# Inverse roots of the keys on GpSimd, and cells and token rows in another order, in a two-layer attention and expert kernel

## The chip, the cores and the metric

The kernel runs on one core of a Trainium2 chip. The metric is the device time of one execution in microseconds (us). Engines are TensorE (PE in the profile, its weight loads PEld), VectorE (DVE), ScalarE (ACT), GpSimd (POOL) and SyncE (SP, which issues most transfers). Everything is float32 unless a row says otherwise.

## The reference, cut to what matters

The input is 8 batches of 256 tokens of 512 values. Layer 0 has attention and a mixture of experts, layer 1 an adapted linear map and a second mixture; each layer adds its result to its input.

```
q, k, v = x @ Wq.T, x @ Wk.T, x @ Wv.T        # 8 query heads, 4 key/value heads, 64 wide
q, k = rope(rms(q, q_scale), pos), rope(rms(k, k_scale), pos)   # rms: x * rsqrt(mean(x*x) + 1e-6) * (1 + scale)
k_blocks, v_blocks = ... .at[block, :, off].set(k), ...set(v)   # new rows go into a paged pool
p = softmax(q @ k_all.T / 16, over the last 256 positions)
y = (p @ v_all) @ Wo.T
# experts of layer 0: one dense matrix W, plus sparse changes for each of 8 experts
deltas   = softmax(expert_atom_weights) @ atoms          # 8 x 4096
weighted = deltas * sigmoid(importance)
vals     = sum over the top 2 experts of rw * weighted   # each of 4096 values belongs to a cell mask_idx of the 512x512 matrix
out      = y @ W.T + segment_sum(y[:, cols] * vals, rows)
```

Layer 1 (a linear map with LoRA adapters, then 8 experts with GELU) is untouched by the change.

## The kernel before, in words

The program is written out by hand, engine by engine; each engine has one queue of instructions in program order and waits on semaphores. There are 16 tiles of 128 tokens, two to a batch.

**Key stage and opening.** TensorE projects tile after tile of x to 256 key and 256 value columns into PSUM bank t mod 8 (line 673) and may reuse a bank once ScalarE has read it out (`kv_nr`). ScalarE squares the keys head by head with a sum (`squares`, line 968). For each pair of tiles VectorE (`sums_k`, line 1376) makes the mean, its reciprocal, ScalarE takes the square root (`roots`, line 973), and VectorE does one Newton step to get `rstd` (last line 1390). ScalarE scales the keys by it and copies the values (`scaled`, lines 981 and 983), VectorE applies the rope (`rope_k`, lines 1397, 1400, 1409), SyncE stores the tile in `new_kv` (line 363). Between the pairs VectorE works on the page tables (`index_work`, lines 1281 to 1372). GpSimd fetches raw weights (lines 505 to 509), then waits for the index of the first batch and for all 16 stores, gathers the rows of batch 0 from the pool (`old_rows`) and from `new_kv` (`new_rows`, line 524, `over_rows`, line 552), and makes the query scales (`scales`, lines 531 to 544): an inverse root by a bit trick and three Newton steps, 15 small operations with a drain after each.

TensorE behind the keys projects query tile 0 into bank 0, multiplies raw weights with the gates (lines 807 to 815), projects query tile 1 into bank 0, forms `deltas` with 128 records on 8 columns into banks 6 and 7 (line 823), turns the query tile and the two halves of the keys (line 679) through bank 0, each copied by ScalarE before the next, and waits for the cell weights of VectorE (`wgt_ok`) and for the weights w_o and w0 (`att_w`). Then the batches begin.

**Batches.** A period of batch B has 8 steps j. TensorE does scores of two (head, tile) pairs (`dots`, line 704), turns probabilities of the pair before (`turn_p`, line 711) and mixes values (`mix`, line 723); it projects queries of the next batch at j = 2 and 4, turns keys of the next batch at j = 6 and 7, and between these projects the attention output. VectorE masks and takes maxima (`tops`, line 1505), scales probabilities (line 1516), ropes the next queries, and routes finished tokens. Bank 0 is shared by all such uses in a fixed order (`uses`), with counters `bk` (written) and `bc` (read out). In batch 0 `cell_sums` (line 743) adds cells that have the same index, and VectorE's `move_cells` takes the sums.

**Cells.** The sparse changes are scattered with an add into `m_buf`, 32 scatters one after the other (`cells`, line 566), 8 each in rounds b = 1 to 4 of GpSimd's loop (line 585). The same loop gathers rows of batch b + 1, makes its query scales, and sends token rows of finished batches to the experts' buffer (`send`, line 558). SyncE fetches `m_buf` back in 16 pieces into two buffers (`fetch_m`, line 371), the first two after the second query projection of batch 5 and after all 32 scatters; VectorE adds them to the dense matrix (`add_cells`, line 1534), one half piece in each step from j = 3 of batch 5 on. After batch 7 the additions left over are done, then both layers' experts run.

The cell values need `atoms`, which lie where the rows of batch 1 go; so GpSimd waits for `delta` before it gathers those.

## Time and profile before

| | us |
|---|---|
| median of 3 runs | 1119.12 (1115.15 to 1119.79) |
| the profiled execution | 1120.77 |
| its span, first to last instruction | 1119.0 |
| TensorE busy | 944.0 (84%) |
| VectorE busy | 556.6 (50%) |
| ScalarE busy | 418.8 (37%) |
| GpSimd busy | 329.0 (29%) |
| mean granted TensorE clock | 0.932 of full speed |

Times in rows are microseconds from the span's start, lengths of one instruction in a group are ns. In a timeline a row has start, length, engine, line, operation, what it writes and reads, how often, and in brackets the idle time of its engine just before and what ended it. SPq is SyncE's queue. A float32 product of TensorE shows as two records.

### The profile page before, as it was taken

Reading aid. Unit: us, or ns where it says so; the run is one execution under the profiler, and the core shown is the slowest. Engines: PE = TensorE matmul, PEld = TensorE weight load, DVE = VectorE, ACT = ScalarE, POOL = GpSimd, SP = SyncE. Lnnn points to the kernel's source line nnn. Section 1 sums busy time; section 2 is a strip of 40 time slices with the busy share of each in tenths; the row PEclk is TensorE's granted clock in tenths of the full one; section 3 lists DMA queues with packets and bytes.
Section 4 is the critical chain, followed back from the end, with each engine's and each line's share of the span. In section 5 each row is a group of like instructions: output and inputs, shape, how many; then the busy total and the mean of one; then the engine's idle time right before and its main releaser. Section 6 shows DMA issues by size and latency. Waiting matters only on the chain.

```text
span 1119.0 us, 18432 instructions
## 1 busy us (share of the span) xinstructions
PE 944.0 (84%) x4690; PEld 609.2 (54%) x4691; DVE 556.6 (50%) x2242; ACT 418.8 (37%) x1283; POOL 329.0 (29%) x368
## 2 busy tenths in 40 slices
PE   6995799888986798706989996999199999999994
PEld 2463475454543454403434444888077777777772
DVE  4678757675753878563333442455333333333331
ACT  3452645554543555301111111222144444555440
POOL 3003215646553152111333441133212212212221
PEclk9986989999999899967999998999689999999998
DMA  8947314244234243357777774794643333333330
GB/s 283 301 189 256 106 39 127 66 115 118 69 87 133 78 137 132 114 167 213 205 209 158 136 125 132 283 395 170 195 113 63 67 67 69 69 67 68 61 58 1
DMA packets 76552, 152.12 MB, mean 136 GB/s; under 512 B 15719, under 2 KB 24599, under 8 KB 74832
## 3 DMA queue, kind: packets, MB, share of 16 engines
q1 hardware_dynamic: 38624, 84.87, 23.0%
q0 software_dynamic: 25520, 45.11, 19.7%
q10 hardware_dynamic: 12352, 21.51, 5.8%
q8 instruction: 20, 0.33, 0.1%
q14 instruction: 36, 0.29, 0.1%
HBM read 94.05 MB, written 69.00 MB: 146 GB/s over the span
## 4 chain that ended last, share of the span: by engine, by line
PE 62%; DVE 11%; DMA 10%; issue 9%; ACT 3%; DVEq 2%; SPq 1%; another core or an unknown queue 1%; POOL 0%; ACTq 0%; POOLq 0%
PE ps L657 50%; DMA acc<-R,tok_i 5%; PE ps L663 4%; PE ps L723 3%; DVE R L1516 2%; DVE R L1534 2%; PE ps L711 2%; DVE R L1505 1%; ACT R L1011 1%; DMA R<-acc 1%; DMA R<-rows 1%; PE ps L704 1%; DMA rows<-zrow 1%; DMA R<-m_buf 1%; PE ps L743 1%
## 5 line engine op out<-in xcount | busy, mean ns | idle before, releaser
L657 PE MATMUL ps<-R 128*128 128x128 f32 (+4 forms) x2768 | 689.3, 405 | 38.5 <-issue 19.6
L657 PEld LDWEIGHTS ps<-R 128*128 128x128 f32 x2768 | 421.2, 195 | 266.4 <-issue 251.2
L629 POOL DMA_INDIRECT out_x<-R,tok_i x39 | 60.5, 1551 | 252.5 <-DVEq L1859 156.9
L663 PE MATMUL ps<-ident,R 128*128 128x128 f32 x440 | 67.5, 286 | 75.0 <-DMA R<-rows 59.7
L663 PEld LDWEIGHTS ps<-ident,R 128*128 128x128 f32 x440 | 53.7, 147 | 108.9 <-issue 94.0
L1022 ACT ACTIVATE R<-R,nmx 128x384 f32<-128x384 f32 x128 | 78.3, 621 | 84.1 <-DVE nmx L1505 71.5
L558 POOL DMA_INDIRECT rows<-R,slot_i x64 | 65.0, 1015 | 141.0 <-DVEq L1608 62.9
L629 POOL DMA_INDIRECT acc<-R,tok_i x39 | 60.9, 1561 | 134.4 <-DVE R L1768 131.3
L1505 DVE CUSTOM_DVE_ANT_0 R<-ps,R,q_scale 128x384 f32<-128x384 f32 x128 | 73.6, 612 | 41.1 <-issue 41.1
L711 PE MATMUL ps<-ident,R 128*128 128x128 f32 x384 | 57.2, 285 | 34.3 <-DVE R L1516 22.6
L1181 ACT ACT_TABLE_LOAD x18 | 23.1, 1283 | 147.8 <-PE ps L657 147.8
L711 PEld LDWEIGHTS ps<-ident,R 128*128 128x128 f32 x384 | 43.6, 145 | 60.1 <-DVE R L1516 34.9
L1173 ACT ACTIVATE R<-R 128x2048 f32 x39 | 75.4, 1937 | 1.5 <-issue 1.5
L1854 DVE TENSOR_TENSOR R<-ps,R 128x512 f32<-128x512 f32 x39 | 27.0, 691 | 95.9 <-PE ps L657 95.9
L1106 ACT ACTIVATE R<-ps 128x512 f32<-128x512 f32 x39 | 23.3, 597 | 108.8 <-PE ps L663 103.4
L566 POOL DMA_INDIRECT m_buf<-tot,cell_i x32 | 51.4, 1605 | 37.2 <-DMA m_buf<-tot,cell_i 21.8
L704 PE MATMUL ps<-R 64*128 64x384 f32 x256 | 61.3, 559 | 0.8 <-ACT R L999 0.8
L1028 ACT ACTIVATE R<-ps 128x384 f32<-128x384 f32 x128 | 56.5, 506 | 5.9 <-PE ps L711 5.9
L1516 DVE TENSOR_SCALAR R<-R,rsum 128x384 f32<-128x384 f32 x128 | 49.4, 427 | 5.6 <-issue 0.9
L1181 ACT ACTIVATE R<-ps,inv_f 128x128 f32<-128x128 f32 x156 | 44.6, 377 | 18.4 <-PE ps L657 18.2
L723 PE MATMUL ps<-R 128*64 128x256 f32 x384 | 51.0, 403 | 0.0
L1834 DVE COPY R<-ps 128x512 f32<-128x512 f32 x39 | 25.3, 686 | 51.1 <-PE ps L663 51.1
(292 smaller groups left out, 901.0 us busy)
## 6 DMA issues: line engine op xcount, KB each, us to landing
R<-rows SPq DMA_DIRECT2D x78, 258.0 KB, 3.1
R<-in_fc ACTq DMA_DIRECT2D x16, 1024.0 KB, 5.6
m_buf<-R SPq DMA_DIRECT2D x8, 1024.0 KB
R<-m_buf SPq DMA_DIRECT2D x16, 512.0 KB
R<-acc SPq DMA_DIRECT2D x32, 256.0 KB
R<-in_x_t SPq DMA_DIRECT2D x4, 1024.0 KB, 10.9
R<-in_x_t SPq DMA_DIRECT2D x8, 512.0 KB, 3.6
new_kv<-R SPq DMA_DIRECT2D x16, 256.0 KB, 2.0
```

The source lines that it names most:

```text
L558: po.indirect_dma_start(out=rows_d, out_offset=bass.IndirectOffsetOnAxis(ap=slot_i[:, c, t:t + 1], axis=0), in_=rows[:, t, :], in_offset=N ...
L629: po.indirect_dma_start(out=sums[s], out_offset=bass.IndirectOffsetOnAxis(ap=tok_i[:, s:s + 1], axis=0), in_=y_sb[s], in_offset=None, boun ...
L657: m = pe.matmul(out, lhs(k), rhs(k), start=(k == 0 and first), stop=(k == KC - 1 and last))
L663: m = pe.transpose(out[:, k * P:(k + 1) * P], src[:, k * P:(k + 1) * P], ident[:])
L704: pe.matmul(ps[:, 2 + u % 4, 0:KW], q_t[s][base:base + 64, jj, qt * P:(qt + 1) * P], k_t[s][base:base + 64, p, qt * P:qt * P + KW], start= ...
L711: m = pe.transpose(ps[:, 6 + u % 2, c * P:(c + 1) * P], prob[u % 4][:, c * P:(c + 1) * P], ident[:])
L723: n = pe.matmul(ps[HD * x:HD * (x + 1), 1, KC // 2 * P * (m % 2):KC // 2 * P * (m % 2 + 1)].rearrange("p (i q) -> p i q", q=P), kv[s][:, q ...
L1022: ac.activation(prob[u % 4], msk_s[u % 4], ACT.Exp, bias=nmx[:, u:u + 1], scale=-1.0, accum_out=sums[:, u:u + 1]).then_inc(S["s_exp"], 1)
L1173: ac.activation(fc1_s[s], fc1[:, :, e, :], ACT.Copy).then_inc(S2["k_w"][s], 1)
L1181: g = ac.activation(h_t[s][:, c, :], ps[:, 2 + s, c * P:(c + 1) * P], ACT.Gelu, bias=b1_t[:, e, c:c + 1])
L1505: ve.tensor_tensor_reduce(out=msk_s[u % 4], in0=ps[:, 2 + u % 4, 0:KW], in1=mask[:, u // NH, :], scale=q_scale[:, B % 2, u:u + 1], scalar= ...
L1516: TS(prob[u % 4], prob[u % 4], rsum[:, u % NH:u % NH + 1], None, ALU.mult).then_inc(S["s_sc"], 1)
```

## The change

1. Keys' roots: `sums_k` and `roots` are gone. GpSimd makes `rstd` for a pair of tiles (`key_roots`) with the same steps as the query scales (`inverse_roots`, 14 operations). ScalarE squares one pair ahead of the pair that it scales; `ss` and `rstd` have four slots instead of two.
2. GpSimd's queue: pairs 0 and 1 stand ahead of the raw-weight transfers, pairs 2 to 7 ahead of everything else, with the gathers of batch 0's old rows behind pair 5.
3. Query tile 1 is projected straight behind query tile 0, into bank 2; the two key turns of the opening go to banks 3 and 4.
4. The 128 records of `deltas` move from the opening to the first two steps of batch 0 (bank 1), VectorE's cell weights to step 1 of batch 0. The wait for w_o and w0 moves to batch 1.
5. VectorE's `index_work` and `sparse_eq` are spread in another way over the key stage.
6. GpSimd's loop over batches: three scatters go ahead of the scales, three go between the row transfers behind them. SyncE asks for the first two pieces of `m_buf` after the stores of batch 4 instead of after the second query projection of batch 5.

```diff
@@ SyncE
-            sp.wait_ge(S["bk"], uses(-1)["p1"] + 1)
+            sp.wait_ge(S["o_p1"], 1)
             load_q(1)
...
                     load_q(b + 2)
-                if b == 5:
-                    sp.wait_ge(S["mscat"], 16 * ST)
-                    for m in range(2):
-                        fetch_m(m)
                 sp.wait_ge(S["s_pv"], 4 * b + 2)
                 sp.dma_start(a0[b], x0[b]).then_inc(S["acc_z"], 16)
...
+                if b == 4:
+                    sp.wait_ge(S["mscat"], 16 * ST)
+                    for m in range(2):
+                        fetch_m(m)
@@ GpSimd
+            def inverse_roots(src, out, k):
+                x, y, t = nw_x[:, 0:k], nw_y[:, 0:k], nw_t[:, 0:k]
+                po.tensor_scalar(x, src, 1.0 / HD, RMS_EPS, ALU.mult, ALU.add)
+                po.drain()
+                po.tensor_scalar(y.bitcast(I32), x.bitcast(I32), -0.5, 1597463007.0, ALU.mult, ALU.add)
+                po.drain()
+                for n in range(3):
+                    po.tensor_tensor(t, y, y, ALU.mult)
+                    po.drain()
+                    po.tensor_tensor(t, t, x, ALU.mult)
+                    po.drain()
+                    po.tensor_scalar(t, t, -0.5, 1.5, ALU.mult, ALU.add)
+                    po.drain()
+                    po.tensor_tensor(out if n == 2 else y, y, t, ALU.mult)
+                    if n < 2:
+                        po.drain()
+            def key_roots(n):
+                r = slice(2 * (n % 2), 2 * (n % 2) + 2)
+                po.wait_ge(S["kv_sq"], 2 * n + 2)
+                wait(po, S["kv_nr"], 2 * n - 2)
+                inverse_roots(ss[:, r].rearrange(flat), rstd[:, r].rearrange(flat), 2 * NG)
+                po.drain().then_inc(S["rst"], 2)
+            for n in range(2):
+                key_roots(n)
             po.wait_ge(S["w_kv"], 16)
...
-            po.wait_ge(S["idx_ok"], 1)
-            old_rows(0)
+            for n in range(2, NT // 2):
+                key_roots(n)
+                if n == 5:
+                    po.wait_ge(S["idx_ok"], 1)
+                    old_rows(0)
...
-            po.wait_ge(S["delta"], 1)
+            po.wait_ge(S["delta"], 2)
             old_rows(1)
...
+                if add:
+                    for n in range(2, 5):
+                        cells(t + n)
+                if b + 1 < NB:
+                    scales(b + 1)
                 for n in range(4):
                     if b >= 2:
                         ...
                         send(a_rows, 2 * b - 4 + n // 2, n % 2, S["xs_sc"])
-                    if add:
-                        cells(t + 2 + n)
-                if b + 1 < NB:
-                    scales(b + 1)
-                if add:
-                    cells(t + 6)
-                    cells(t + 7)
+                    if add and n < 3:
+                        cells(t + 5 + n)
@@ TensorE
+            def cell_deltas(x):
+                if x == 0:
+                    pe.wait_ge(S["pre_c"], 1)
+                    pe.wait_ge(S["atoms_d"], 32)
+                for t in range(ST // 2 * x, ST // 2 * (x + 1)):
+                    for y in range(2):
+                        m = pe.matmul(ps[64 * y:64 * y + 64, 1, t * NE:(t + 1) * NE], ...)
+                m.then_inc(S["delta"], 1)
...
+                    if j == 0 and first:
+                        pe.wait_ge(bc, uses(-1)["q0"] + 1)
+                        pe.wait_ge(S["o_kc"], 2)
+                        pe.wait_ge(S["q_rp"], 2)
...
+                        if B == 1:
+                            pe.wait_ge(S["att_w"], 16 * (2 * KC + 1))
...
                     dots(B, j, s)
+                    if j < 2 and first:
+                        cell_deltas(j)
...
             project_q(opening, 0)
+            pe.wait_ge(S["kv_nr"], NT - 5)
+            queries(1, 2).then_inc(S["o_p1"], 1)
             pe.wait_ge(S["raw_dma"], 16 * 5)
-            pe.wait_ge(S["kv_nr"], NT - 6)
...
-            project_q(opening, 1)
...
             for p in range(2):
-                turn_k(opening, p, 0)
-            pe.wait_ge(S["wgt_ok"], 1)
-            pe.wait_ge(S["att_w"], 16 * (2 * KC + 1))
+                turn_k4(ps[:, 3 + p, :], 0, p).then_inc(S["o_k"], 1)
@@ ScalarE
+            for t in range(2):
+                squares(t)
+            for n in range(NT // 2):
+                for t in (2 * n + 2, 2 * n + 3):
+                    if t < NT:
+                        squares(t)
+                for t in (2 * n, 2 * n + 1):
+                    scaled(t)
@@ VectorE
+            for n in range(NT // 2):
                 for x in range(2):
                     rope_k(2 * n + x)
+                if n in (0, 1, 2, 3, 4):
+                    next(index)
+                if n in (2, 4):
+                    next(index)
+                if n == 5:
+                    tables(0, tabq_a, tabq_b)
+                if n == 6:
+                    sparse_eq(0, 4)
...
             rope_q(0)
-            sparse_eq(0, 8)
             rope_q(1)
             outside(0)
             build_mask(0)
-            cell_weights()
+            sparse_eq(4, 8)
```

## Rows read from the trace of the kernel before

**Rows 1.** The chain of waits, opening; start, length, what.

```profile
82.28 13.62 issue
95.90 5.79 PE ps L657 x8
101.69 7.16 PE ps L823 x126
```

**Rows 2.** Timeline of TensorE, key stage and opening.

```profile
10.73 60.64 PE L657 MATMUL ps<-R 128*128 128x512 f32 x136 [10.73 <-DMA R<-in_x_t]
...
110.67 1.09 PE L679 MATMUL ps<-ident,R 128*128 128x128 f32 x4 [0.78 <-ACT R L999]
...
114.34 2.93 PE L704 MATMUL ps<-R 64*128 64x384 f32 x8 [0.78 <-ACT R L999]
...
118.93 0.88 PE L711 MATMUL ps<-ident,R 128*128 128x128 f32 x6 [1.06 <-DVE R L1516]
```

**Rows 3.** Timelines of ScalarE and VectorE, first squares and last keys.

```profile
19.75 0.20 ACT L968 ACTIVATE R<-ps 128x64 f32<-128x64 f32 x1
...
88.14 0.93 ACT L981 ACTIVATE R<-ps,rstd 128x64 f32<-128x64 f32 x4 [1.02 <-DVEq L1391]
...
87.91 0.16 DVE L1390 TENSOR_TENSOR rstd<-rstd,root 128x4 f32<-128x4 f32 x1
...
90.55 0.42 DVE L1409 TENSOR_TENSOR R<-R 128x256 f32<-128x256 f32 x1
```

**Rows 4.** Timeline of GpSimd, key stage and opening.

```profile
19.99 0.98 POOL L505 DMA_DIRECT2D gate<-in_gate_t  x1 [12.81 <-DMA R<-in_x_t]
...
23.22 0.78 POOL L509 DMA_DIRECT2D R<-in_b_o  x1
...
94.53 0.94 POOL L524 DMA_INDIRECT R<-new_kv,new_idx  x1 [44.05 <-DVEq L1371]
...
98.81 1.55 POOL L552 DMA_INDIRECT R<-new_kv,new_idx  x1 [0.30 <-issue]
...
105.67 0.60 POOL L533 TENSOR_SCALAR nw_y<-nw_x 128x16 int32<-128x16 int32 x1 [1.48 <-issue]
...
112.03 0.27 POOL L544 TENSOR_SCALAR q_scale<-nw_y 128x16 f32<-128x16 f32 x1 [0.16 <-issue]
```

**Rows 5.** Timeline of GpSimd, batches 4 and 5.

```profile
314.81 0.98 POOL L558 DMA_INDIRECT rows<-R,slot_i  x1 [0.30 <-issue]
316.19 1.58 POOL L566 DMA_INDIRECT m_buf<-tot,cell_i  x1 [0.40 <-DMA m_buf<-tot,cell_i]
...
320.99 0.29 POOL L533 TENSOR_SCALAR nw_y<-nw_x 128x16 int32<-128x16 int32 x1 [2.44 <-issue]
...
325.83 0.26 POOL L544 TENSOR_SCALAR q_scale<-nw_y 128x16 f32<-128x16 f32 x1 [0.16 <-issue]
...
330.28 1.56 POOL L566 DMA_INDIRECT m_buf<-tot,cell_i  x1 [1.65 <-DMA m_buf<-tot,cell_i]
...
372.15 0.98 POOL L536 TENSOR_TENSOR nw_t<-nw_y 128x16 f32<-128x16 f32 x1
```

**Rows 6.** Timeline of VectorE, batch 5.

```profile
372.02 1.09 DVE L1534 TENSOR_TENSOR R<-R 128x512 f32<-128x512 f32 x1
```

**Rows 7.** Timelines of VectorE and TensorE and the chain of waits, batch 5.

```profile
363.18 1.07 DVE L1534 TENSOR_TENSOR R<-R 128x512 f32<-128x512 f32 x1 [13.43 <-DMA R<-m_buf]
...
364.88 1.54 PE L711 MATMUL ps<-ident,R 128*128 128x128 f32 x6 [7.20 <-DVE R L1516]
...
358.13 5.02 DMA R<-m_buf
```

**Rows 8.** Timeline of SyncE's queue, the stores of batches 4, 5 and 6.

```profile
321.17 0.52 SPq L393 DMA_DIRECT2D acc<-in_x  x1
...
373.46 0.53 SPq L393 DMA_DIRECT2D acc<-in_x  x1
...
417.01 0.52 SPq L393 DMA_DIRECT2D acc<-in_x  x1
```

More of the change, by code:

```diff
@@ L117, in program @@
         nrm = [words(R2, 14336 + KD * s, [KD]) for s in range(2)]
-        sq = [words(R2, 14848 + KD * s, [KD]) for s in range(2)]
+        sq = [words(R2, base, [KD]) for base in (14848, 15104, 5120, 5376)]
         sin_t = words(R2, 15360, [NT, HD // 2])
@@ L206, in program @@
         tot = sb("tot", [P, ST, NE])
-        ss = sb("ss", [P, 2, NG])
-        rstd = sb("rstd", [P, 2, NG])
-        root = sb("root", [P, 2, NG])
+        ss = sb("ss", [P, 4, NG])
+        rstd = sb("rstd", [P, 4, NG])
         ssq = sb("ssq", [P, 16])
@@ L719, in mix @@
                     wait(pe, S["s_ot"], 2 * B + qt)
+                if B == 0 and m == 0:
+                    pe.wait_ge(S["wgt_ok"], 1)
                 for c in range(3):
@@ L963, in squares @@
             def squares(t):
[L964 removed]
                 ac.wait_ge(S["kv_mm"], t + 1)
[L966 removed]
+                wait(ac, S["rst"], 2 * (t // 2) - 2)
                 for h in range(NG):
[L968 removed]
+                    c = ac.activation(sq[t % 4][:, h * HD:(h + 1) * HD], ps[:, t % 8, h * HD:(h + 1) * HD], ACT.Square, accum_out=ss[:, t % 4, h:h + 1])
                 c.then_inc(S["kv_sq"], 1)
[L971 to L974 removed]
             def scaled(t):
[L977 to L978 removed]
+                ac.wait_ge(S["rst"], 2 * (t // 2) + 2)
                 wait(ac, S["p1r"], t - 1)
                 for h in range(NG):
[L981 removed]
+                    ac.activation(nrm[t % 2][:, h * HD:(h + 1) * HD], ps[:, t % 8, h * HD:(h + 1) * HD], ACT.Copy, scale=rstd[:, t % 4, h:h + 1])
                 wait(ac, S4["p1k"][t % 4], 16 * (t // 4))
                 ac.activation(kv_out[t % 4][:, KD:D], ps[:, t % 8, KD:D], ACT.Copy).then_inc(S["kv_nr"], 1)
[L985 to L994 removed]
+            for t in range(2):
[6 more added lines that the diff above has]
+                    scaled(t)
             bk, bc = S["bk"], S["bc"]
@@ L1077, in _ @@
             ac.activation(lora_b[:, D:DG], ps[:, 1, 128:128 + NE], ACT.Copy).then_inc(S["pre_c"], 1)
[L1078 removed]
             q_out(opening, 0, 0)
             for p in range(2):
[L1081 removed]
+                ac.wait_ge(S["o_k"], p + 1)
+                copy_bank(3 + p, k_t[0][:, p, :]).then_inc(S["o_kc"], 1)
             periods(ac, period)
@@ L1414, in rope_q @@
                 ve.wait_ge(S["q_ss"], t + 1)
-                rope(ps[:, 0, :], rq_a, rq_b, tabq_a, tabq_b, NH, t).then_inc(S["bc"], 1)
+                last = rope(ps[:, 2 if t == 1 else 0, :], rq_a, rq_b, tabq_a, tabq_b, NH, t)
+                if t != 1:
+                    last.then_inc(S["bc"], 1)
                 ve.drain()
@@ L1432, in _ @@
             next(index)
-            sums_k(0, 0, BOTH)
-            for n in range(NT // 2 - 1):
-                if n < 6:
-                    next(index)
-                if n == 6:
-                    tables(0, tabq_a, tabq_b)
-                if n + 1 < NT // 2 - 1:
-                    sums_k(n + 1, 2 * n + 2, BOTH)
-                else:
-                    sums_k(n + 1, NT - 2, (0,))
+            for n in range(NT // 2):
                 for x in range(2):
                     rope_k(2 * n + x)
-            sums_k(NT // 2, NT - 2, (1,))
-            for x in range(2):
-                rope_k(NT - 2 + x)
-            next(index)
+                if n in (0, 1, 2, 3, 4):
[6 more added lines that the diff above has]
+                    sparse_eq(0, 4)
             def cell_weights():
@@ L1669, in period @@
                         build_mask(1)
+                    if j == 1 and first:
+                        cell_weights()
                     if j == 2 and not last:
```

96 lines of the change are left out of this document (25 added, 71 removed).

## The prediction

> **What bounds the kernel now.** I read the chain of waits first, then the timelines of the engines in the opening, then the waits of the batches. Up to 71 us TensorE is never idle: 136 records of key and query products run back to back [rows 2], so nothing that speeds up the keys' normalisation can shorten that part. What the other engines owe at its end is the price. TensorE has done the products of the raw weights at 82.28 and then stands for 13.62 us [rows 1]: the second query projection wants bank 0, which VectorE frees only after the ropes of all keys, and these trail. The last inverse root is ready at 87.91 + 0.16 = 88.1, the last key is roped at 90.97 [rows 3], GpSimd starts its four gathers of new rows at 94.53 [rows 4]. From there everything is serial: projection, cell products (7.2 us), turns of the queries and keys through one bank, first scores at 114.34, first turned probabilities at 118.93 [rows 1, 2]. A second hole is in batch 5: VectorE waits 13.43 us for the first piece of `m_buf`, since SyncE asks for it only after the second query projection of that batch; TensorE is idle for 7.20 us in it [rows 7]. Behind batch 7 (experts, layer 1) the change touches no instruction.
>
> **Step 1, the key stage with its roots on GpSimd.** Before, each pair went ScalarE, VectorE, ScalarE (root), VectorE, with VectorE's index work in the same queue. Now VectorE and ScalarE give up their part (9 times six VectorE and one ScalarE instructions of about 0.2 us; this pays nothing in itself, TensorE covers it), and GpSimd has 14 small operations with drains per pair. A quiet run of the same code is 13 intervals from 320.99 to 325.83, 0.37 us each [rows 5], so a pair costs c = 14 x 0.37 = 5.2 us when nothing disturbs it. The disturbed run in the opening took from 105.67 to 112.30 for 14 operations, 6.6 us [rows 4]. I take c = 5.8, since VectorE's ropes of two SBUF operands fill roughly half of the time.
> GpSimd's queue is now in this order: pairs 0 and 1, the five raw-weight transfers (19.99 to 24.0, 4.0 us [rows 4]), pairs 2 to 5, two gathers (half of the four that took 94.53 to 100.36 [rows 4], 2.9), pairs 6 and 7. After a transfer the first drain costs: the second operation comes 3.2 us after the last issue ended (317.77 to 320.99 [rows 5]). That is twice 3.2. The first pair can begin when its eight squares of 0.20 are there, 19.75 + 1.6 = 21.3 [rows 3]. So the last roots are ready at R = 21.3 + 8c + 4.0 + 2.9 + 6.4 = 34.6 + 8c: 76.2 for 5.2, **81.0 for 5.8**, 87.4 for 6.6. TensorE is not held up by it: its last key product needs pair 3, the first query projection pair 4, the second pair 5, and these are ready more than 5 us earlier at c = 5.8. Raw weights asked for some 13 us later are still wanted only at 75 us.
>
> **Step 2, from R to the first probabilities.** Scaling tile 14 on ScalarE takes 0.93 and a copy, 1.2 [rows 3]; the two ropes run 2.7: stored at R + 3.9. From there to the gathers 3.6 (90.97 to 94.53 [rows 3, 4]), four gathers 5.8: R + 13.3. Then the query scales: 3.2 for the first drain, 5.1 for the rest [rows 5]: R + 21.6 is where VectorE can start on scores. The squares of both query tiles no longer hold them, because the second projection now runs at 71 to 75, into bank 2, at the rate of the key products (8 of 136 records in 60.64 us, 3.6) instead of the 5.79 at 95.90 [rows 1, 2]. Beside that TensorE: the last gather lands about 1.7 after its issue (as a scatter does, 1.65 [rows 5]), R + 15.0; two key turns of 1.1 into two banks and one copy of 0.8 [rows 2]: R + 18.0. Then, new on this path, the cell products: scores 1.5, half of 7.2, scores 1.5, the other half, a query turn 1.0 [rows 1, 2]: the first probabilities are turned at **R + 29.2**. The scales at R + 21.6 hide behind that. Before it was 118.93. So the opening gives 89.7 - R: **8.7 us** at c = 5.8, 13.5 at 5.2, 2.3 at 6.6. Of the rest, VectorE's cell weights move behind the products that they need, its eight comparisons are split four before and four after the last ropes (I price them with the spread of c), and SyncE's 1 MB weight transfer, waited for only in batch 1, is off the path. Rows for batch 1 are gathered later relative to batch 0, after the cell products, but are wanted in its step 6, some 35 us on.
>
> **Step 3, the fetch moved from batch 5 to the end of batch 4.** SyncE issues two transfers of 512 KB after the stores of batch 4 (321.17 [rows 8]) as soon as all 32 scatters are in; behind that wait stands only the last query load, which follows a projection of batch 5 that was over at 357.7 (the end of what the fetch waited for [rows 7]). In GpSimd's new order three scatters go before the scales and three after, between the row transfers. In the times of before: scales done at 326.1, a row transfer of 1.0 with a gap of 0.3, then three scatters at 3.3 each, the other row transfers in their shadow: the last one lands at about 338.3 (before 331.8 + 1.6 [rows 5]). The first piece takes 5.0 from issue [rows 7]: 343.3, against 349.75 when VectorE asks for it (363.18 - 13.43 [rows 7]). Six us of margin, so the wait goes. It isn't worth its 13.43: TensorE was partly ahead. The mark of the stores tells: batch 4 to 5 took 52.29 us, batch 5 to 6, with more additions in it, 43.55 [rows 8]. **8.7 us.** Ends: 6.0 (TensorE's idle time less the gap of about a us that is there in other batches) and 13.4. What is late next is the ordinary pace of a batch, VectorE with additions and scales.
> The scales of the next batch are nowhere later: they wait for the squares at 318.35 (320.99 less 2.44 and 0.20) in either order [rows 5]. Token rows go out after them, and are wanted only after batch 7.
>
> **Sum.** The profiled execution took 1120.8 (span 1119.0). 1120.8 - 8.7 - 8.7 = 1103.4. The median of the runs shown, 1119.1, lies 1.7 lower, so I say **1102**.
>
> **Rivals.**
> GpSimd and VectorE get in each other's way. In batch 5 a GpSimd product of normally 0.22 us lasted 0.98, from 372.15 to 373.13, and VectorE's addition of two SBUF operands ran from 372.02 to 373.11 [rows 5, 6]: it ended with it. If each of the 14 operations waits out one rope instruction of 0.42 [rows 3], c = 5.2 + 5.9 = 11.1, R = 123.4, the opening loses 33.7, and the time is 1120.8 + 33.7 - 8.7 = 1146. Slower by over 0.5% needs R above 104, c above 8.7. For it: the same engines are now busy in the same stage. Against: ropes are in bursts with waits between, and of the batches' scale runs most operations were undisturbed. 4 in 100. The Trainium skill (SBUF — State Buffer, SBUF: two separate sides) says that the pair of ports which both engines use is locked exclusively for a whole instruction when VectorE has two SBUF inputs; by that rule as the full case c would be near 11 and the sum 1146; the trace agrees on the lock and not on its happening each time.
> The middle of it: c about 6.6, the roots end where they ended before, the opening gives only 2. Then 1120.8 - 2.3 - 8.7 = 1109.8, or 1108 by the median. 13 in 100.
> The opening is better: drains after transfers cost little and c = 5.2. The floor of R is the last squares, one projection ahead of TensorE's 71.4 and 0.9 more, so 69, and 5.2: 74, a gain of 15.7; with c = 5.2 alone it is 13.5. At 15, 1120.8 - 15 - 8.7 = 1097, 1095 by the median. 13 in 100.
> The scatters are late, because rows share their queue, and VectorE still waits in batch 5: only the opening's 8.7 is left, 1112, 1110 by the median. Against it the six us of margin. 7 in 100.
> Neither does what it says, a gather or a store that lands late under the weight transfers takes the place of the roots, and batch 5 hides its hole otherwise: 1119. 4 in 100.
> My forecast, both steps within their bounds, has 59 in 100.
>
> **The numbers.** About 0.5%, 5.6 us, is what a measurement of this kernel tells from no change; 1113.5 is that bound. Forecast, the middle case, the better opening and most of the late-scatter case lie below: 0.90. Same 0.06, slower 0.04. Range: the forecast's ends (8.7 by 2.3 to 13.5, 8.7 by 6 to 13.4) and the neighbouring rivals give 1093 to 1112.
>
> **What would show it.** In the profile after: TensorE without a gap over 2 us up to 75, last ropes near 85 instead of 91; GpSimd's runs of 14 operations at 5 to 6.5 us; probabilities first turned near 110; cell products between the first scores; in batch 5 no wait of VectorE for `m_buf`, and 43 to 45 us between the stores of batches 4 and 5. Wrong if a GpSimd run takes over 7 us, if TensorE waits in the key stage, if the chain in batch 0 passes through a gather of batch 1, or if everything from batch 1 on isn't the same length as before.

## The result, and the profile after

| | before | after |
|---|---|---|
| median of 8 runs each, side by side | 1118.01 us (1114.08 to 1119.79) | 1106.47 us (1102.52 to 1111.22) |
| span of the profiled execution | 1119.0 | 1104.9 |
| GpSimd busy | 329.0 | 358.8 |
| mean granted TensorE clock | 0.932 | 0.933 |

The ratio is 0.9911, interval 0.9886 to 0.9936: 11.5 us faster. The prediction said 1102 and 17 us. The total is in its range, but hardly a part of it came where it was put. The mark of SyncE's first store of each batch shows that; all marks of before stand in [rows 8] or in the same view (140.13 for batch 0, 188.71 for batch 1):

| stretch | before | after | gained |
|---|---|---|---|
| start to the stores of batch 0 | 140.13 | 151.18 | -11.05 |
| batch 0 to 1 | 48.58 | 48.35 | 0.23 |
| batch 1 to 4 (three batches) | 132.46 | 121.11 | 11.35 |
| batch 4 to 5 | 52.29 | 40.05 | 12.24 |
| batch 5 to the end | 745.54 | 744.21 | 1.33 |
| the whole span | 1119.0 | 1104.9 | 14.1 |

The opening, predicted to gain 8.7 us, lost 11. The fetch, predicted at 8.7, stands in a stretch that gained 12.2. And batches 1 to 4, priced at nothing, gained 11.4.

**The opening.** GpSimd's timeline of the kernel after, around its raw-weight transfers (start, length, and in brackets the idle time before):

```profile
33.70 0.20 POOL L516 TENSOR_TENSOR rstd<-nw_y,nw_t 128x8 f32<-128x8 f32 x1
35.98 0.99 POOL L534 DMA_DIRECT2D gate<-in_gate_t  x1 [2.08 <-issue]
...
39.24 0.77 POOL L538 DMA_DIRECT2D R<-in_b_o  x1
40.09 0.26 POOL L505 TENSOR_SCALAR nw_x<-ss 128x8 f32<-128x8 f32 x1
55.70 0.20 POOL L507 TENSOR_SCALAR nw_y<-nw_x 128x8 int32<-128x8 int32 x1 [15.36 <-issue]
```

The transfers of the same stretch (35 to 60 us: size, median us from issue to landing):

```profile
R<-in_w POOLq DMA_DIRECT2D x1, 1024.0 KB, 15.1
...
R<-in_b_o POOLq DMA_DIRECT2D x1, 256.0 KB, 16.1
```

The last transfer was issued at 39.24 and landed 16.1 us later, at 55.3; the drain between the first and second operation of pair 2 ended at 55.70. The timing fits a drain that waits until GpSimd's own transfers have landed (raw_sp, rows_behind and gather_first below test it); they share the DMA engines here with a megabyte of zeros and the stores. TensorE's timeline of the kernel after shows what hangs on that:

```profile
61.49 23.21 PE L678 MATMUL ps<-R 128*128 128x512 f32 x48 [7.28 <-ACT R L1017]
84.63 10.36 PE L678 MATMUL ps<-gate,R 128*64 128x8 f32 x104
94.92 0.27 PE L864 MATMUL ps<-ident,R 8*128 8x8 f32 x1
105.49 1.11 PE L684 MATMUL ps<-ident,R 128*128 128x128 f32 x4 [10.29 <-DVE R L1442]
115.83 1.94 PE L700 MATMUL ps<-ident,R 128*128 128x128 f32 x8 [9.23 <-DMA R<-new_kv,new_idx]
118.50 1.65 PE L729 MATMUL ps<-R 64*128 64x384 f32 x4 [0.73 <-issue]
120.08 3.69 PE L773 MATMUL ps<-eaw_t,R 64*64 64x8 f32 x64
...
129.82 1.49 PE L736 MATMUL ps<-ident,R 128*128 128x128 f32 x6
```

TensorE stands 7.28 us inside the key stage, which before had no gap [rows 2]: no bank was free, because no key could be scaled. The first probabilities are turned at 129.82; before it was 118.93. Further down GpSimd's queue:

```profile
84.03 0.22 POOL L507 TENSOR_SCALAR nw_y<-nw_x 128x8 int32<-128x8 int32 x1 [2.60 <-issue]
...
93.43 0.94 POOL L510 TENSOR_TENSOR nw_t<-nw_y 128x8 f32<-128x8 f32 x1
...
96.36 0.77 POOL L516 TENSOR_TENSOR rstd<-nw_y,nw_t 128x8 f32<-128x8 f32 x1
104.14 1.02 POOL L553 DMA_INDIRECT R<-new_kv,new_idx  x1 [7.00 <-DMA new_kv<-R]
...
116.01 0.21 POOL L507 TENSOR_SCALAR nw_y<-nw_x 128x16 int32<-128x16 int32 x1 [6.51 <-issue]
```

The last roots are ready at 97.13 (81.0 predicted); four operations of pair 7 took 0.76 to 0.94 instead of 0.20, beside VectorE's comparisons of cell indices; and the four gathers landed only 6.6 us after issue (the median; the last one took 7.6), so that the next drain took 6.51. TensorE's turn of the keys, which the landing of the last gather releases, starts at 115.83, and the operation behind the drain at 116.01. In the six kernels of "The opening, taken apart" these two stand 0.17 to 0.26 us apart as well.

**The fetch.** SyncE's timeline of the kernel after, batch 4 to 5 (before, the fetch stood behind the query projection of batch 5 and VectorE waited 13.43 us for it [rows 7]):

```profile
320.64 0.52 SPq L388 DMA_DIRECT2D acc<-in_x  x1
...
338.34 1.06 SPq L370 DMA_DIRECT2D R<-m_buf  x2
```

It goes out at 338.34, 17.7 us behind the mark of batch 4. The prediction had 338.3, which is 17.1 behind the mark of before. No wait of VectorE for `m_buf` is left in that batch.

### The profile page after: what moved, and what is told of

It reads as the page before. It is cut to its first block, busy times and chain, and to the rows that moved or that the text cites. A ratio compares the mean times of both kernels' runs of the same rounds, so it can differ in the third digit from the quotient of the medians.

```text
span 1104.9 us, 18551 instructions
## 1 busy us (share of the span) xinstructions
PE 936.2 (85%) x4690; PEld 607.2 (55%) x4691; DVE 546.7 (49%) x2188; ACT 415.6 (38%) x1273; POOL 358.8 (32%) x480
## 4 chain that ended last, share of the span: by engine, by line
PE 54%; DVE 13%; issue 12%; DMA 9%; POOLq 4%; DVEq 2%; ACT 2%; SPq 1%; POOL 1%; ACTq 0%
PE ps L678 43%; DMA acc<-R,tok_i 5%; PE ps L684 4%; PE ps L750 2%; DVE R L1534 2%; DVE R L1552 2%; DVE R L1523 2%; PE ps L736 1%; DMA R<-acc 1%; ACT R L1042 1%; DMA rows<-zrow 1%; PE ps L729 1%; DMA R<-rows 1%; PE ps L783 1%; DMA R<-new_kv,new_idx 1%
## 5 line engine op out<-in xcount | busy, mean ns | idle before, releaser
L678 PE MATMUL ps<-R 128*128 128x128 f32 (+4 forms) x2768 | 684.9, 404 | 23.3 <-DMA R<-in_x_t 10.5
L736 PE MATMUL ps<-ident,R 128*128 128x128 f32 x384 | 56.8, 283 | 22.8 <-DVE R L1534 12.2
L1144 ACT ACTIVATE R<-ps 128x512 f32<-128x512 f32 x39 | 23.3, 597 | 109.9 <-PE ps L684 107.6
L1031 ACT ACTIVATE R<-ps 128x512 f32<-128x512 f32 x48 | 28.5, 594 | 54.2 <-PE ps L684 39.5
```

The costliest lines, as they stand in the source:

```text
L678: m = pe.matmul(out, lhs(k), rhs(k), start=(k == 0 and first), stop=(k == KC - 1 and last))
L736: m = pe.transpose(ps[:, 6 + u % 2, c * P:(c + 1) * P], prob[u % 4][:, c * P:(c + 1) * P], ident[:])
```

## The experiments

Each ratio is to the kernel before, run beside it on the same chip; its median there was 1118 to 1126 us, so the ratios are what to compare. "Marks" are the stores of the batches, as in the table.

### One part of the change at a time

**fetch_only.** The kernel before with the move of the fetch alone:

```diff
-                if b == 5:
-                    sp.wait_ge(S["mscat"], 16 * ST)
-                    for m in range(2):
-                        fetch_m(m)
                 sp.wait_ge(S["s_pv"], 4 * b + 2)
                 sp.dma_start(a0[b], x0[b]).then_inc(S["acc_z"], 16)
...
+                if b == 4:
+                    sp.wait_ge(S["mscat"], 16 * ST)
+                    for m in range(2):
+                        fetch_m(m)
```

> The kernel before, with one edit: SyncE asks for the first two pieces of m_buf after the stores of batch 4 instead of in batch 5. Theory (the fetch gives what the prediction said): VectorE's wait of 13.43 us in batch 5 goes, the stores of batch 5 come 43 to 44 us after those of batch 4 instead of 52.3, and the time falls by 8 to 9 us. Rival (part of it was paid by other things, such as the faster batches of the changed kernel): it falls by less than 5. In both, batches 2 to 4 keep their 43.7 to 44.5 us each.

Measured: 1112.92 us, ratio 0.9894 (0.9855 to 0.9934). Batch 4 to 5 took 41.3 us instead of 52.29, batches 1 to 4 stayed at 43.1 to 43.9 each:

```profile
322.09 0.52 SPq L389 DMA_DIRECT2D acc<-in_x  x1
...
334.33 1.07 SPq L371 DMA_DIRECT2D R<-m_buf  x2
...
363.38 0.53 SPq L389 DMA_DIRECT2D acc<-in_x  x1
```

The fetch is worth 11.0 us by the marks.

**order_only.** The kernel before with the new order of GpSimd's loop alone:

```diff
+                if add:
+                    for n in range(2, 5):
+                        cells(t + n)
+                if b + 1 < NB:
+                    scales(b + 1)
                 for n in range(4):
...
-                    if add:
-                        cells(t + 2 + n)
-                if b + 1 < NB:
-                    scales(b + 1)
-                if add:
-                    cells(t + 6)
-                    cells(t + 7)
+                    if add and n < 3:
+                        cells(t + 5 + n)
```

> The kernel before, with one edit: GpSimd's loop has three scatters ahead of the query scales and the row transfers behind them. Theory A (the row transfers, or a transfer behind them, disturb TensorE in step 3 and 4 of batches 2 to 4, where it resumes 2.6 us late and then runs at half clock): batches 2 to 4 take 40 to 41 us each instead of 43.7 to 44.5, some 11 us less by batch 5, where VectorE's wait for m_buf stays, so the time falls by 9 to 12. Theory B (the batches of the changed kernel are faster for another reason, say the later opening): batches 2 to 4 stay at 44 and the time within 2 us.

Measured: 1109.67 us, ratio 0.9862 (0.9822 to 0.9902). Batches 1 to 4 at 40.70, 41.09 and 40.13 us: 10.5 us less than in before. Batch 4 to 5 stayed at 51.0. So the order of transfers, the part priced at zero, is worth about as much as the fetch: 10.5 against 11.0 us by the marks, and the intervals of the two ratios overlap.

**order_fetch.** Both, with the old opening.

> The kernel before with both of these edits and its old opening, so neither roots on GpSimd nor moved cell products. If the opening of the changed kernel costs what its trace shows (first probabilities turned at 129.8 against 118.9), this is some 11 us faster than the changed kernel: about 1096, 20 us or more under the kernel before. If the late opening is made up for later, it is within 3 us of the changed kernel.

Measured: 1097.74 us, ratio 0.975 (0.9704 to 0.9795). By the medians the two gains add up (15.1 and 11.9 against 27.1 us), the first probabilities come at 118.06, and this kernel, without the new opening, beats the changed one.

### What the order of transfers removes

Before, in batches 2 to 4, there is a stall that [rows 5] show only from GpSimd's side. TensorE and then ScalarE in batch 3 of the kernel before:

```profile
262.25 1.99 PE L657 MATMUL ps<-R 128*128 128x256 f32 x8
264.18 0.92 PE L704 MATMUL ps<-R 64*128 64x384 f32 x4
267.39 5.37 PE L657 MATMUL ps<-R 128*128 128x512 f32 x8 [2.29 <-issue]
```

```profile
266.86 0.38 ACT L1017 ACTIVATE R<-ps 128x256 f32<-128x256 f32 x1 [4.70 <-remote]
```

The same steps in order_only, TensorE and ScalarE:

```profile
261.20 1.99 PE L657 MATMUL ps<-R 128*128 128x256 f32 x8
263.12 0.92 PE L704 MATMUL ps<-R 64*128 64x384 f32 x4
263.97 3.70 PE L657 MATMUL ps<-R 128*128 128x512 f32 x8
```

```profile
263.23 0.38 ACT L1017 ACTIVATE R<-ps 128x256 f32<-128x256 f32 x1 [1.77 <-PE ps L657]
```

ScalarE reads the product 0.04 us behind its modelled end in order_only and 2.6 us behind it in before. VectorE, which waits for the scores, is late by about the same time (2.5 us). Then the query projection starts at the lower clock (granted 0.50 from 268 to 270, the 1.2 GHz level; 1.00 in order_only) and takes 5.37 instead of 3.70 us. Together 4.3 us in this batch (2.6 and 1.67); by the marks it is 3.5 per batch (44.15 on average in batches 1 to 4 against 40.64). In before the first row transfer of the round is issued at 261.34, 5.5 us ahead of ScalarE's late start. Three orders of the same ten transfers were tried on the kernel before.

**sends_behind.** The four scatters stay ahead of the scales, the four rows go behind them.

```diff
+                if add:
+                    for n in range(4):
+                        cells(t + 2 + n)
+                if b + 1 < NB:
+                    scales(b + 1)
                 for n in range(4):
...
                         send(a_rows, 2 * b - 4 + n // 2, n % 2, S["xs_sc"])
-                    if add:
-                        cells(t + 2 + n)
-                if b + 1 < NB:
-                    scales(b + 1)
```

> The kernel before; in GpSimd's loop the four scatters of the middle stay ahead of the query scales, and only the four transfers of token rows go behind the scales (before: row, scatter, row, scatter ... scales). Opening and fetch as before. Theory A (in batches 2 to 4 the token rows ahead of the scales, beside the scatters, go with the stall of 2.6 us and the slow query projection): the stores of batches 1 to 4 stand 40 to 41 us apart as in order_only, and the time is 8 to 13 us below before, ratio near 0.987. Rival B (it is the number of scatters ahead of the scales, three instead of four, that counts, or their landing): the stores stay 43 to 44.5 us apart and the time is within 3 us of before.

Measured: 1127.49 us, ratio 1.0043 (1.0029 to 1.0057). The stall is gone everywhere and batch 1 to 2 takes 40.86 us, as theory A says; but the next ones take 45.36 and 47.67. The trace suggests another reason. Four scatters in a row each wait for the landing of the one before, rows no longer fill that time, and with the rows and two scatters behind them the next round starts late. GpSimd's last operation of the scales in this kernel:

```profile
246.05 0.26 POOL L544 TENSOR_SCALAR q_scale<-nw_y 128x16 f32<-128x16 f32 x1 [0.16 <-issue]
```

That is 15.6 us behind the mark 230.41; in before it is 6.0 (239.18 against 233.17), in order_only 4.8.

**scatter_first.** Scatter and row change places in each of the four pairs.

```diff
                 for n in range(4):
+                    if add:
+                        cells(t + 2 + n)
                     if b >= 2:
...
                         send(a_rows, 2 * b - 4 + n // 2, n % 2, S["xs_sc"])
-                    if add:
-                        cells(t + 2 + n)
```

> The kernel before; in GpSimd's loop scatter and row transfer change places in each of the four pairs ahead of the scales (scatter, row, scatter, row ... instead of row, scatter, ...), so that the first row goes out some 3 us later in the batch. In before TensorE's signals to ScalarE and VectorE come 2.6 us late in batches 2 to 4 shortly behind the first row transfer, and the next query projection runs 5.36 instead of 3.70 us. Theory A (any token rows ahead of the scales bring the stall, wherever they stand): the stall is there again in batches 2 to 4, moved by up to 3 us or at the same step, stores 43.5 to 44.5 us apart, the time within 3 us of before. Rival B (it needs the row transfer at that very moment, beside a fetch of instructions at 217 or 261): the stall is gone in most batches, stores 40 to 41.5 apart, the time 6 to 12 us below before.

Measured: 1124.24 us, ratio 0.9996 (0.9968 to 1.0024). No stall of 2.6 us in batches 2 to 4, although rows still go ahead of the scales; every query projection takes 3.70. Batches 1 to 4 took 40.80, 45.64 and 40.92 us, batch 4 to 5 56.7. The gain is given back in the same way: 15.2 us behind the mark 231.63 the scales are ready, and VectorE's first masking of the batch (L1505) starts only then:

```profile
246.81 0.26 POOL L544 TENSOR_SCALAR q_scale<-nw_y 128x16 f32<-128x16 f32 x1 [0.16 <-issue]
```

```profile
247.17 0.61 DVE L1505 CUSTOM_DVE_ANT_0 R<-ps,R,q_scale 128x384 f32<-128x384 f32 x1 [2.07 <-issue]
```

**rows_alone.** The four rows ahead of the scales, all six scatters behind.

```diff
                         send(a_rows, 2 * b - 4 + n // 2, n % 2, S["xs_sc"])
-                    if add:
-                        cells(t + 2 + n)
                 if b + 1 < NB:
                     scales(b + 1)
                 if add:
-                    cells(t + 6)
-                    cells(t + 7)
+                    for n in range(2, 8):
+                        cells(t + n)
```

> The kernel before; ahead of the scales only the four row transfers, and all six scatters of the middle behind the scales. Theory A (the rows bring the stall): batches 2 to 4 show the late signals of 2.6 us and a projection over 5 us, the stores stay 43 to 44.5 us apart; time within 4 us of before. Rival B (the stall comes from scatters that alternate with rows): no stall, stores 40 to 41 us apart in batches 1 to 4. In both the scatters end later, so that the wait for m_buf in batch 5 may grow by a few us.

Measured: 1125.68 us, ratio 1.0021 (0.9989 to 1.0054), marks 43.67, 40.19 and 45.54 us apart. In rounds 2 to 4 of GpSimd's loop the late signals are back, now at another step, and in batch 3 to 4 the scales are late as well, 14.5 us behind the mark. The first row of batch 3's round is issued at 272.93, and ScalarE's timeline has:

```profile
279.06 0.60 ACT L997 ACTIVATE R<-ps 128x512 f32<-128x512 f32 x1 [5.20 <-remote]
```

Side by side, the late signals follow a pattern, but not without exception. In before a round's first row goes out directly behind the two gathers of `over_rows` (217.08, 261.34, 305.06, 347.14, 402.72), and 5.3 to 6.3 us later ScalarE's read starts (222.53, 266.86, 310.52, 353.47, 408.06): 2.5, 2.6 and 2.6 us behind the end of the product, then 1.9, and 1.2 in the last of the five:

```profile
408.06 0.38 ACT L1017 ACTIVATE R<-ps 128x256 f32<-128x256 f32 x1 [3.29 <-PE ps L657]
```

In fetch_only all five come again, 3.1 to 1.2 us late. In rows_alone it is 3.0 us in rounds 2 to 4 (in round 2 it is SyncE's store at 233.01 that comes 3.0 us behind the end of the product that it waits for), and none in rounds 5 and 6, though the rows stand there in the same way; in round 5 TensorE is idle at that time. scatter_first has a scatter between gathers and first row in rounds 2 to 4, and no signal 2.5 us late there. In rounds 5 and 6 no scatters are left, the row (350.28 and 404.14) stands behind the gathers, and the signal is 1.6 and 1.1 us late:

```profile
356.36 0.38 ACT L1017 ACTIVATE R<-ps 128x256 f32<-128x256 f32 x1 [3.71 <-remote]
```

But one in its round 4 is late too, by 1.2 us, and it comes ahead of that round's first row (310.92):

```profile
309.24 0.38 ACT L1017 ACTIVATE R<-ps 128x256 f32<-128x256 f32 x1 [3.27 <-PE ps L657]
```

sends_behind, order_only, order_fetch and after never have a row directly behind the gathers, and at this step no signal more than 0.6 us late. So the long delays go with such a row in every case, and short ones come without it. That the row is their cause isn't shown, and what the signal waits for was not found: fetches of instructions stand near the rows in both kinds of kernels.

So two things go with the order. A first row directly behind the gathers goes with 3.5 us lost in a batch by the marks. Scales 14.5 to 17.2 us behind the mark go with some 5 us or more, while at 11.8 and 12.2 a batch took 40.9 us as in order_only. The new order avoids both; sends_behind and scatter_first run into the second and rows_alone into both.

### The opening, taken apart

Each kernel is the one above it with one more edit, and all have the new order and fetch.

**raw_sp.** The kernel after, the five raw-weight transfers asked for by SyncE.

```diff
@@ SyncE, behind the load of mask_bc
+            sp.dma_start(gate0[:], d["gate0_t"].rearrange(chunked, p=P)).then_inc(S["raw_dma"], 16)
...
+            sp.dma_start(raw_b, d["b_o"].rearrange(chunked, p=P)).then_inc(S["raw_dma"], 16)
@@ GpSimd, behind pair 1
-            po.wait_ge(S["w_kv"], 16)
...
-            po.dma_start(raw_b, d["b_o"].rearrange(chunked, p=P)).then_inc(S["raw_dma"], 16)
```

> The changed kernel with one edit: the five raw-weight transfers go out from SyncE's queue, behind the mask indices, instead of from GpSimd's. Theory (a GpSimd drain stands until the transfers of its own queue have landed): the gap of 15.4 us behind the first operation of pair 2 is gone, the pairs follow each other at 5 to 6.5 us, TensorE doesn't wait before 71 us, the last root is ready at 76 to 82 instead of 97.1, first probabilities are turned at 110 to 115 instead of 129.8, and the time is 14 to 20 us below the changed kernel. Rival (the gap comes from the load on the transfer engines or from VectorE): a gap of over 8 us stays and so does the time, within 4 us.

Measured: 1102.23 us, ratio 0.9817 (0.9763 to 0.9871), first probabilities at 123.13 instead of 129.82. Pair 2 starts at 35.12 and runs through; the gap of 15.4 us is gone, as the theory said. But the last roots are ready only at 90.94 (76 to 82 expected) and the first probabilities come 6.7 us earlier, not 15 to 20. ScalarE now waits 9.71 us, to 52.44, for a store that stands behind the raw weights in SyncE's queue, and pair 4 waits for ScalarE. The next gap of the same kind, behind the gathers of old rows, remains too:

```profile
55.63 0.20 POOL L510 TENSOR_SCALAR nw_x<-ss 128x8 f32<-128x8 f32 x1 [8.93 <-ACT R L1004]
...
73.13 0.45 POOL L510 TENSOR_SCALAR nw_x<-ss 128x8 f32<-128x8 f32 x1
78.56 0.20 POOL L512 TENSOR_SCALAR nw_y<-nw_x 128x8 int32<-128x8 int32 x1 [4.99 <-issue]
```

**rows_behind.** The old rows of batch 0 behind pair 7 instead of pair 5.

```diff
             for n in range(2, NT // 2):
                 key_roots(n)
-                if n == 5:
-                    po.wait_ge(S["idx_ok"], 1)
-                    old_rows(0)
+            po.wait_ge(S["idx_ok"], 1)
+            old_rows(0)
```

> The kernel after, raw weights from SyncE's queue (as in raw_sp), and the two gathers of batch 0's old rows behind pair 7 of the key roots instead of between pairs 5 and 6. Theory A (a drain behind a transfer of GpSimd's own queue waits until that transfer has landed): in raw_sp the second operation of pair 6 came 4.99 us after the first; here pair 6 has no such gap, the last roots are ready near 86 instead of 90.94, and the first drain behind the gathers comes with the query scales, where one is paid anyway. Time 2 to 5 us below raw_sp (ratio near 0.978). Rival B (the gap is the cost of a new kind of instruction, or of waiting for ScalarE): pair 6 keeps a gap of 4 us or more and the time is raw_sp's, 0.982. Rival C: the gap goes, but VectorE's index work or the stores hold the last keys, so that the gathers start where they started (97.9) and the time is the same.

Measured: 1096.81 us, ratio 0.976 (0.9726 to 0.9794). No gap in pair 6, the last roots at 81.99, first probabilities at 114.76. The roots come 9 us earlier than in raw_sp, not 5: with the drain's 4.99 the two issues and GpSimd's wait of 2.98 us ahead of them left the chain. The mark of batch 0 comes 8.6 us earlier (144.76 to 136.13); the intervals of the two ratios overlap a little.

**gather_first.** SyncE asks for w_o, w0 and the last zeros only when batch 0 is gathered.

```diff
+            sp.wait_ge(S["o_p1"], 1)
+            load_q(1)
             sp.wait_ge(S["pre_w"], 1)
+            sp.wait_ge(S2["kvd"][0], 64)
             for k in range(KC):
```

> The kernel rows_behind, and SyncE asks for the weights w_o and w0 and for the last zero stores only when the gathers of batch 0 have landed (they are not needed before batch 1; the load of the next queries goes ahead of them). Theory A (the gathers land late because the weights and zeros share the DMA engines; 6.6 us median in the kernel after): the gathers land 2 to 3 us after issue, the second operation of the query scales comes 2 to 3 us after the first instead of 6, TensorE's key turns start 3 to 4 us earlier relative to the gathers' start, and the time is 3 to 4 us below rows_behind. Rival B (the gathers' time is that of the gathers themselves, four of 128 rows one after the other): landing stays above 5 us, the time stays.

Measured: 1090.04 us, ratio 0.9682 (0.9658 to 0.9706). The drain in the scales fell from 4.99 to 1.60 us, TensorE's wait for the gathers from 7.62 to 4.23, first probabilities at 111.54. By the mark of batch 0 the step is worth 3.0 us (136.13 to 133.15); the two ratios, whose intervals don't overlap, differ by more (0.976 and 0.9682).

**eq_late.** VectorE's first four comparisons moved from behind pair 6 to the end of the opening.

```diff
-                if n == 6:
-                    sparse_eq(0, 4)
...
             build_mask(0)
-            sparse_eq(4, 8)
+            sparse_eq(0, 8)
```

> The kernel gather_first, and VectorE's first four comparisons of cell indices moved from behind the ropes of pair 6 to the end of the opening, where the other four stand. Theory A (they hold the ports that GpSimd shares: its products took 0.94, 0.80, 0.76 and 0.77 beside them instead of 0.20): pair 7's roots take 5 us instead of 7.8, the last roots come 2 to 3 us earlier, and the time is 2 us below gather_first unless the comparisons, now 7.6 us together, hold the first scores. Rival B (the long products come from the ropes or from ScalarE's reads): pair 7 keeps products of 0.7 us or more and the time is the same or longer.

Measured: 1086.68 us, ratio 0.967 (0.965 to 0.969). GpSimd's same two operations in pair 7, in gather_first and in eq_late:

```profile
78.16 0.93 POOL L522 TENSOR_TENSOR nw_y<-nw_y,nw_t 128x8 f32<-128x8 f32 x1
79.23 0.79 POOL L516 TENSOR_TENSOR nw_t<-nw_y 128x8 f32<-128x8 f32 x1
```

```profile
77.18 0.20 POOL L522 TENSOR_TENSOR nw_y<-nw_y,nw_t 128x8 f32<-128x8 f32 x1
77.53 0.20 POOL L516 TENSOR_TENSOR nw_t<-nw_y 128x8 f32<-128x8 f32 x1
```

The comparisons made them long. Now seven operations of the query scales last 0.74 to 0.80 beside all eight comparisons, but TensorE's cell products cover that: first probabilities at 108.04.

**raw_spread.** The raw weights go between the first stores, since ScalarE waited 9.72 us at 51.09 for a store that stood behind them in SyncE's queue.

```diff
                 if t in (2, 5, 8, 11):
                     zero_cells(t // 3)
+                if t == 1:
...
+                    sp.dma_start(raw_wo, d["wo"].rearrange(chunked, p=P)).then_inc(S["raw_dma"], 16)
+                if t == 3:
+                    sp.dma_start(raw_w1, d["w1"].rearrange(chunked, p=P)).then_inc(S["raw_dma"], 16)
+                if t == 4:
+                    sp.dma_start(raw_b, d["b_o"].rearrange(chunked, p=P)).then_inc(S["raw_dma"], 16)
```

> The kernel eq_late, with the raw weights asked for between the stores of the new keys (the gates and wo behind the store of tile 1, w1 behind tile 3, b_o behind tile 4) instead of all ahead of the first store. In eq_late SyncE issues them from 29.3 to 43.0, the first store goes out at 43.12, and ScalarE waits 9.72 us for its landing at 51.09, so that pairs 4 to 7 of the key roots run as one chain behind it. Theory A (that wait is what sets the last roots): no wait of ScalarE over 3 us in the key stage, the last roots ready near 76 instead of 78.77, the first turned probabilities near 105.5 instead of 108.04, and the time 2 to 3 us below eq_late, ratio near 0.965. Rival B (the transfers then land late, or the stores beside them do): TensorE waits for raw weights at 74, or the last store lands later, and the time is the same or longer than eq_late's.

Measured: 1087.63 us, ratio 0.9657 (0.9617 to 0.9696). The trace does what was expected: ScalarE waits 2.01 us at most for a store, the last roots are ready at 75.14, first probabilities at 105.51. (One wait of ScalarE over 3 us is left, 3.30 for the last roots themselves.) In the time the step from eq_late is smaller than the intervals.

**deltas_early.** Half of the cell products into TensorE's wait for the gathers, four comparisons into VectorE's wait for the stores.

```diff
             turn_q(opening, 0)
+            cell_deltas(0)
...
-                    if j < 2 and first:
-                        cell_deltas(j)
+                    if j == 0 and first:
+                        cell_deltas(1)
@@ VectorE, ahead of the waits for the last stores
+            sparse_eq(0, 4)
...
-            sparse_eq(0, 8)
+            sparse_eq(4, 8)
```

> The kernel raw_spread, with half of the cell products (3.69 us) put between the turn of the queries and the turns of the keys, where TensorE waits 4.14 us for the gathers of batch 0, the other half behind the first scores; and VectorE's first four comparisons put where it waits for the last stores (80.5 to 84.1), so that only four stand beside the query scales. Theory A (the path to the first probabilities goes through TensorE's two halves of the cell products, and right behind it through the scales): TensorE's wait for the gathers falls under 1 us, the long products of GpSimd's scales go from seven to three or four, the first probabilities are turned at 101.5 to 102.5 instead of 105.51, and the time is 3 to 4 us below raw_spread, ratio near 0.9625. Rival B (something behind it takes the gain back, the cell sums at step 5, or the rows of batch 1 in its key turns): the probabilities come earlier, but the mark of the stores of batch 0 or batch 1 moves by less than 2 us and the time is raw_spread's, 0.9657.

Measured: 1081.09 us (1073.85 to 1088.60), ratio 0.9679 (0.9639 to 0.9719); before beside it was 1119.33. TensorE's timeline:

```profile
86.64 3.69 PE L773 MATMUL ps<-eaw_t,R 64*64 64x8 f32 x64
90.97 1.94 PE L700 MATMUL ps<-ident,R 128*128 128x128 f32 x8 [0.63 <-DMA R<-new_kv,new_idx]
...
101.33 1.48 PE L736 MATMUL ps<-ident,R 128*128 128x128 f32 x6
...
111.90 0.88 PE L736 MATMUL ps<-ident,R 128*128 128x128 f32 x6 [2.84 <-DVE R L1533]
```

The probabilities come at 101.33, 4.2 us earlier, and the long products of the scales are three instead of seven. TensorE then waits 2.84 for VectorE, and the mark of batch 0 moved by 2.5 (125.92 to 123.39), but that of batch 1 by 4.0 (175.71 to 171.76), so that rival B's sign, less than 2 us, didn't come. Still the ratio isn't the 0.9625 that was expected: the gain of the trace is not found in the times, and why stays open. The four ratios from gather_first on lie between 0.9657 and 0.9682 with overlapping intervals, so that the times can't rank these four kernels. All beat both the kernel before and the changed one, by about 3.3% and 2.4%.

## Why the prediction was right in its total and wrong in its parts

**Step 1, roots on GpSimd: wrong, and this is the step that failed.** The cost of a pair was right (4.8 us quiet at 21.59 to 26.35, 6.1 for pair 1, against 5.2 and 5.8). What failed is the term "after a transfer the first drain costs 3.2", and with it that TensorE is not held up by it. 3.2 was read behind a scatter [rows 5] and taken as a price of the drain; the runs make it the time until the own transfers have landed (the trace has no landing for that scatter, so for the 3.2 itself this is inferred). Behind transfers of which two have 1 MB the drain was 15.36, and TensorE stood for 7.28 us. "Raw weights asked for some 13 us later are still wanted only at 75 us" was true of TensorE and missed who waited first. R was 97.1 for 81.0. Of these 16.1 us, 12.5 are that drain (15.7 from the end of the last issue to the second operation, for 3.2) and 2.0 are pair 7 beside VectorE's comparisons (7.8 for 5.8); the rest are short waits. The second drain, behind the old rows, was as priced (3.05).

**Step 2, from R on: 32.7 us for 29.2.** The stores and the gathers' start were right (R + 7.0 for R + 7.5). The four gathers were taken to land 1.7 after issue, like a scatter; they took 6.6, since w_o, w0 and the zeros, which no longer held TensorE, now ran beside them. Key turns came at R + 18.7 instead of R + 15.0. gather_first gives these 3.4 us back.

**Step 3, the fetch: right in mechanism, low in size.** 8.7 with ends 6.0 and 13.4; fetch_only moved the stretch by 11.0.

**The loop's order, priced at zero: wrong.** "The scales of the next batch are nowhere later" was true, and nothing else was asked. The trace of before held the hint: 44 us between the marks of batches 1 to 4, with a query projection of 5.37 where its neighbours took 3.70. The prediction costed what the new order does to GpSimd's own work and gave no reason for putting the rest at nothing.

**The sum.** 8.7 + 8.7 + 0 was predicted. The stretches gave -11.1, +12.2 and +11.4 and 1.6 for the rest. So the sum's errors were -19.8, +3.5, +11.4 and +1.6, and only 3.3 us of them is left in the total. That the total lies in the range is luck: a loss of 11 us in the opening was cancelled by a gain of 11.4 us that was not forecast.

**The rivals.** The port lock (c = 11.1) didn't come as the full case: it cost four operations some 0.6 us each. The Trainium skill (SBUF — State Buffer, SBUF: two separate sides) gives the lock for a VectorE instruction with two SBUF inputs; by that rule the trace agrees for the comparisons (0.93 against 0.20 with and without them), while most operations beside the shorter ropes stayed under 0.5. The rival "a gather or a store that lands late under the weight transfers" was named and given 4 in 100; a part of it came true. The late scatters didn't come. Of the signs listed, "wrong if TensorE waits in the key stage" and "if everything from batch 1 on isn't the same length as before" both came.

## What to carry to other kernels

Small dependent operations with drains don't belong behind transfers in GpSimd's own queue: in these runs the drain ended only when they had landed, so either another queue asks for them, or they stand where nothing on the path follows. A new order of transfers in a loop is never free to assume: look for stretches of before where a step is longer than its twin in other batches, and ask which transfer goes with it. And when a total comes out right, compare the marks stage by stage before the reasons are believed.

## What the runs showed of the hardware

- A drain on GpSimd ended with the landing of its own transfers: 15.36 us behind transfers that landed 15.1 and 16.1 us after issue (after), 2.60 to 6.51 behind gathers (after and raw_sp), 1.60 when w_o, w0 and the last zeros no longer ran beside the gathers (gather_first). With the same transfers in SyncE's queue the gap of 15.36 was gone (raw_sp).
- TensorE's clock in the opening of the kernel after: after 10.29 and 9.23 us of waiting with 1.1 us of work between, the windows show the lower level, 1.2 GHz (columns: stretch, its length, busy time of PE, PEld, DVE, ACT and POOL, granted clock, DMA share, GB/s). The same scores take 1.65 us there and 0.92 later.

```profile
115.00:125.00 10.00, 8.44 (x80) 6.21 (x80) 2.54 (x10) 3.79 (x7) 3.05 (x14) 0.50 0.97 405
...
135.00:145.00 10.00, 9.19 (x43) 4.54 (x42) 9.41 (x30) 5.98 (x30) 2.01 (x2) 1.00 0.13 36
```

- Signals of TensorE came 2.5 to 3.1 us late 4.7 to 6.4 us after a row transfer that GpSimd issued directly behind gathers, in rounds 2 to 4 of before, fetch_only and rows_alone, and 1.1 to 1.9 us late in rounds 5 and 6 of before, fetch_only and scatter_first. Without such a row the longest delay at that step was 1.2 us (scatter_first, 309.24). The cause wasn't found.
